# The 32 scatters of routed rows in pairs, each pair waiting until the pair before has landed

## The chip, the cores and the metric

The kernel runs on one core of a Trainium2 chip. The metric is the device time of one execution in microseconds (us); the kernel before was timed three times, and the median is what the changed kernel is held against. The profile is that of one further execution, recorded instruction by instruction.

## The reference

Two gated layers follow each other on 8 x 256 tokens of 128 numbers. The change touches the last part of the second layer, the mixture of experts:

```
x  = x + s0 * silu(local_attention_ffn(layernorm(x)))        # layer 0, s0 from a linear recurrence
xn = layernorm(x)
s  = attention(xn)                                           # 16 heads of 8, causal
probs = softmax(xn @ router_w.T + router_b);  top_w, top_e = top_k(probs, 2);  top_w /= sum(top_w)
for each expert e of 16:                                     # F = 256
    h = silu(xn @ w1[e].T) * (xn @ w3[e].T);  y = h @ w2[e].T
    yn = layernorm(y) * ln_g[e] + ln_b[e]
    out += where(top_e == e, top_w, 0).sum(-1) * yn
x  = x + s * silu(out)
```

Every token thus needs two of the 16 experts, and the kernel computes only these.

## The kernel before

The 2048 tokens are 16 tiles of 128 (`NT = 16`). The program has three parts. **Part a** goes through four turns of four tiles: layer 0, and beside it the second layer's attention of the turn before. **Part b** (the section `LAST` of the planner's order) does the second layer's attention for the last turn, transposes the weights of the 16 experts as they are loaded, and works out the routing. **Part c** takes 48 tiles of 128 routed rows (`CT = 48`) through the experts. Between the parts all engines meet: each drains and adds one to `b_over`, and goes on when it has reached 4.

The hand-over from part b to part c goes through device memory. `XG` (`xg_scratch`) has 48 x 128 places for rows. VectorE (DVE) works out, for every token and each of its two experts, the place of its row, and writes these 32 columns of indices to `POSU` (line 1718). GpSimd (POOL) then copies each token's normalized row to its two places: 16 tiles times 2 indirect DMAs of 128 rows, 64 KB each (lines 1944 to 1947). Each adds 16 to the semaphore `scattered` when it has landed. Nothing of POOL's work follows in part b but its drain; all its other work of part b is queued ahead of the scatters. POOL's queue is in program order.

The queue of SyncE (SP) issues the loads of the expert weights in part b, three of 128 KB per expert into a ring of four (lines 808 to 812). Each next expert waits until TensorE (PE) has transposed the expert four before it. Then it issues two loads of 1 MB (line 814), waits until all 32 scatters have landed (line 817) and until part b is over on all engines (line 818), and loads the rows back from `XG` (line 824); PE's first instructions of part c wait for that load. So whichever ends last in part b, PE's and DVE's chain (which ends in the matmuls "dests" and the cast to `DEST`, lines 1651 to 1653) or POOL's scatters, sets the start of part c.

In part c POOL scatters the experts' outputs to a second scratch, `YT` (`yt_scratch`), one indirect DMA of 64 KB for each of the 48 tiles (line 1918). In part b the order of the items on PE, ScalarE (ACT), DVE and POOL comes from a planner; it ranks the routing step that writes the indices as if 45 us of work stood behind it (`PLACED, SENDING`, lines 130 and 312), which stands for the scatters. The change leaves that as it is. A helper (line 1208) issues all of ACT's activations and another (line 841) many of the matmuls, so that their rows share a line; lines 884 and 926 are the transposes of the attention's probabilities and their products with the values, line 1136 and 1143 the transposes of expert weights.

Of the kernel before, what the change touches and what calls it, by code (L numbers as in the profile page):

```python
# [485 lines left out]
def gated_layers(nc, ins, out):  # L486
    ctx = ExitStack()
    with ctx:
# [3 lines left out]
        def sem(name):  # L492
            return ctx.enter_context(nc.semaphore(name))
# [191 lines left out]
        zeroed, scattered = sem("zeroed"), sem("scattered")  # L685
# [1127 lines left out]
        def _(pool):  # L1813
# [128 lines left out]
            pool.wait_ge(zeroed, 16 * CT // 4)  # L1942
            pool.wait_ge(pos_done, 1)
            for t in range(NT):
                for k in range(2):
                    G.indirect_dma_start(XG, bass.IndirectOffsetOnAxis(POSU[:, k, t:t + 1], 0), XN1ALL[:, t, :], None)\
                        .then_inc(scattered, 16)
# [56 lines left out]
```

## Time and profile before

| | us |
|---|---|
| three runs | 882.73, 886.46, 886.53 |
| median | 886.46 |
| span of the profiled execution, first to last instruction | 918.4 |
| that span less the median | 31.9 |

No other time of the profiled execution is recorded than its span; what lies around a span (start and end of a program) comes on top. The profiled execution was therefore at least 31.9 us longer than the median of the timed ones, which is 3.6%. Busy shares of the span: PE 77%, DVE 70%, ACT 54%, POOL 43%. These are means over three parts with different limits; the part that the change touches runs from about 680 us to 795 us of the span, and is read from its own rows. Times below are from the start of the span.

### The profile page before, as it was taken

The numbers are of one execution on the slowest core, as the hardware profiler recorded it, in microseconds if no ns is written. First come the engines' busy times: TensorE is split into PE (matmuls) and PEld (weight loads), VectorE is DVE, ScalarE is ACT, GpSimd is POOL, SyncE is SP. The second block draws the span as 40 slices with busy tenths as digits, with TensorE's granted clock in tenths as the row PEclk, the third lists the DMA queues.
The fourth block names the chain that finished last, engine by engine and source line by source line (L and its number), as shares of the span: only waits on it lengthen the run. The fifth ranks groups of instructions, "written<-read, shape, count | busy, mean of one in ns | idle before, by whom it ended". The sixth has DMA issues, their size and how long they took to land.

```text
span 918.4 us, 20712 instructions
## 1 busy us (share of the span) xinstructions
PE 708.3 (77%) x7336; PEld 530.8 (58%) x7351; DVE 642.1 (70%) x1521; ACT 496.9 (54%) x893; POOL 392.0 (43%) x470
## 2 busy tenths in 40 slices
PE   4688887689899867998997798999859309798830
PEld 1456554457676734676675466658646207698830
DVE  5586776697869775977986797787658325476645
ACT  2444555465666753656676566655726205487711
POOL 7351633560714063434412760480041750068880
PEclk9789999899999997999999999999978759799975
DMA  8600000000000000000000000000023313122104
GB/s 206 177 1 1 1 1 1 1 1 3 1 2 1 2 1 3 2 1 2 1 2 1 1 1 2 1 2 2 1 87 87 119 42 128 36 70 70 62 35 146
DMA packets 43839, 30.03 MB, mean 33 GB/s; under 512 B 7650, under 2 KB 41692, under 8 KB 43484
## 3 DMA queue, kind: packets, MB, share of 16 engines
q1 hardware_dynamic: 39932, 23.17, 8.7%
q0 software_dynamic: 2560, 5.25, 1.5%
q8 instruction: 64, 1.05, 0.5%
q10 hardware_dynamic: 1248, 0.28, 0.2%
q14 instruction: 35, 0.29, 0.1%
HBM read 18.98 MB, written 9.44 MB: 31 GB/s over the span
## 4 chain that ended last, share of the span: by engine, by line
PE 38%; DVE 24%; issue 13%; POOL 13%; ACT 6%; another core or an unknown queue 4%; DMA 1%; DVEq 1%; POOLq 0%; ACTq 0%; SPq 0%
PE psM L841 14%; DVE arena L1538 5%; PE psO L926 4%; ACT arena L1208 4%; DVE PR L1426 4%; PE psT L884 4%; POOL yt_scratch L1918 3%; PE psS L875 3%; PE psS L911 3%; POOL arena L1895 3%; POOL arena L1892 3%; POOL RS L1871 2%; DVE MX L1420 2%; DVE arena L1546 2%
## 5 line engine op out<-in xcount | busy, mean ns | idle before, releaser
L841 PE MATMUL psM<-arena 128*128 128x128 f32 (+7 forms) x1168 | 267.9, 372 | 44.1 <-DVE arena L1538 25.3
L1208 ACT ACTIVATE arena<-psT 128x512 f32<-128x512 f32 (+2 forms) x296 | 150.8, 530 | 153.9 <-PE psT L1003 37.1
L841 PEld LDWEIGHTS psM<-arena 128*128 128x128 f32 (+5 forms) x1168 | 155.5, 190 | 93.0 <-DVE arena L1538 38.1
L1208 ACT ACTIVATE arena<-psM 128x512 f32<-128x512 f32 (+2 forms) x168 | 88.3, 543 | 114.3 <-PE psM L841 113.3
L1420 DVE TENSOR_REDUCE MX<-psS 128x4 f32<-128x512 f32 (+1 forms) x160 | 102.7, 682 | 62.5 <-issue 24.0
L1870 POOL TENSOR_SCALAR RS<-MV 128x2 f32<-128x2 f32 x56 | 14.4, 256 | 293.2 <-DVE MV L1574 167.5
L1892 POOL TENSOR_TENSOR arena<-arena,powm 128x8 f32<-128x8 f32 x64 | 109.9, 1717 | 5.3
L1208 ACT ACTIVATE PR<-PR 128x512 f32<-128x512 f32 x160 | 94.6, 626 | 21.1 <-DVE PR L1426 20.9
L1426 DVE TENSOR_TENSOR PR<-psS,MX 128x512 f32<-128x512 f32 x160 | 102.1, 678 | 0.0
L884 PE MATMUL psT<-ident,PR 128*128 128x128 f32 x640 | 94.3, 282 | 5.4 <-ACT PR L1208 1.9
L884 PEld LDWEIGHTS psT<-ident,PR 128*128 128x128 f32 x640 | 74.9, 145 | 34.1 <-issue 27.0
L1895 POOL TENSOR_TENSOR arena<-arena 128x512 f32<-128x512 f32 x64 | 85.7, 1339 | 0.0
L1538 DVE TENSOR_TENSOR arena<-psM,arena 128x512 f32<-128x512 f32 x128 | 81.7, 679 | 0.0
L1208 ACT ACTIVATE arena<-arena 128x768 f32 (+3 forms) x61 | 46.6, 763 | 49.9 <-DVE arena L1806 30.0
L1546 DVE TENSOR_TENSOR arena<-arena 128x512 f32<-128x512 f32 x64 | 55.1, 878 | 15.3 <-POOL arena L1895 15.2
L1891 POOL TENSOR_SCALAR arena<-arena 128x8 f32<-128x8 f32 x64 | 17.9, 280 | 104.6 <-DVE arena L1525 104.3
L1208 ACT ACT_TABLE_LOAD x43 | 55.2, 1283 | 10.0 <-PE psT L965 9.3
L1525 DVE TENSOR_REDUCE arena<-arena 128x8 f32<-128x512 f32 x64 | 43.4, 678 | 21.0 <-ACT arena L1208 20.6
L1003 PE MATMUL psT<-ident,arena 128*128 128x128 f32 x256 | 40.8, 287 | 19.9 <-DVE arena L1546 19.8
L911 PE MATMUL psS<-arena 32*128 32x256 f32 (+1 forms) x512 | 55.7, 346 | 0.0
L1918 POOL DMA_INDIRECT yt_scratch<-arena,DEST x48 | 49.7, 1036 | 12.1 <-issue 7.3
L1906 POOL TENSOR_SCALAR arena<-arena,lanem 128x256 f32<-128x256 f32 x32 | 29.2, 934 | 55.8 <-ACT arena L1208 55.8
(198 smaller groups left out, 1163.8 us busy)
## 6 DMA issues: line engine op xcount, KB each, us to landing
arena<-in_L_ffn_w SPq DMA_DIRECT2D x50, 128.0 KB
xg_scratch<-zeros SPq DMA_DIRECT2D x12, 256.0 KB, 3.7
arena<-xg_scratch SPq DMA_DIRECT2D x12, 256.0 KB
arena<-yt_scratch SPq DMA_DIRECT2D x4, 512.0 KB, 5.3
arena<-in_L_ffn_wqkv SPq DMA_DIRECT2D x2, 768.0 KB, 5.0
arena<-in_L_ffn_ln_g SPq DMA_DIRECT2D x1, 1024.0 KB, 5.3
arena<-in_L_ffn_ln_b SPq DMA_DIRECT2D x1, 1024.0 KB, 8.5
out<-arena SPq DMA_DIRECT2D x4, 256.0 KB, 2.2
```

What stands on the lines that cost most here:

```text
L841: return nc.tensor.matmul(o, lhsT, rhs, start=start, stop=stop)
L884: last = nc.tensor.transpose(bank[:, c * P:(c + 1) * P], PR[:, m % 4, c * P:(c + 1) * P], ident[:])
L911: last = nc.tensor.matmul(Sb[i][:, c * keys:(c + 1) * keys], QL[r, b, lane, qt * P:(qt + 1) * P], KT1[r, b * SEQ:b * SEQ + keys], start=False,
L1208: return nc.scalar.activation(o, i, f, **kw)
L1420: V.tensor_reduce(maxima[i], scores[i], AX, ALU.max).then_inc(dstep, 1)
L1426: V.tensor_tensor(PR[:, (n + i) % 4, :].rearrange("p (s k) -> p s k", s=ns), scores[i], maxima[i].unsqueeze(2).broadcast_to([P, ns, 512 // ...
L1525: V.tensor_reduce(SS[:, m % 4, :], SQ[:, m % 2, :].rearrange("p (h d) -> p h d", h=8), AX, ALU.add).then_inc(ss_done.sem(m), 1)
L1538: last = V.tensor_tensor(dst.rearrange("p (h d) -> p h d", h=8), src, RT[:, 2 * l + n % 2, x, t % 2, :].unsqueeze(1) .broadcast_to([P, 8, ...
L1546: V.tensor_tensor(r1, r1, RN[:, m % 4, :].unsqueeze(2).broadcast_to([P, 8, DH]), ALU.mult)\
L1892: G.tensor_tensor(RN[:, m % 4, :], RN[:, m % 4, :], powm[:, 0:8], ALU.pow)
L1895: G.tensor_tensor(r1, r1, r2[:, :, ::-1, :], ALU.add).then_inc(rope_sum.sem(m), 1)
L1918: G.indirect_dma_start(YT, bass.IndirectOffsetOnAxis(DEST[:, tile:tile + 1], 0), YO[:, tile % OUT_RING, :], None)\
```

## The change

Ahead of the two scatters of every tile but the first, POOL waits until all scatters issued so far have landed. Nothing else differs.

```diff
             pool.wait_ge(zeroed, 16 * CT // 4)
             pool.wait_ge(pos_done, 1)
             for t in range(NT):
+                if t:
+
+                    pool.wait_ge(scattered, 16 * 2 * t)
                 for k in range(2):
                     G.indirect_dma_start(XG, bass.IndirectOffsetOnAxis(POSU[:, k, t:t + 1], 0), XN1ALL[:, t, :], None)\
                         .then_inc(scattered, 16)
```

On POOL, at the scatters, the difference of the two orders is this (the names are those of the section above; the scatters' line is 1949 in the changed kernel; the piece stops after the third pair):

```order
 L1906 TENSOR_SCALAR arena<-arena,lanem 128x256 x3
-L1946 DMA xg_scratch<-XN1ALL,POSU 6144x128 [waits pos_done,zeroed]
-L1946 DMA xg_scratch<-XN1ALL,POSU 6144x128 x31
+L1949 DMA xg_scratch<-XN1ALL,POSU 6144x128 [waits pos_done,zeroed]
+L1949 DMA xg_scratch<-XN1ALL,POSU 6144x128
+L1949 DMA xg_scratch<-XN1ALL,POSU 6144x128 [waits scattered]
+L1949 DMA xg_scratch<-XN1ALL,POSU 6144x128
+L1949 DMA xg_scratch<-XN1ALL,POSU 6144x128 [waits scattered]
```

No instruction moved; the first scatter of each of 15 pairs now carries a wait, where 31 scatters stood without one.

On SP, at the end of part b, this stands in both kernels, and it is who waits for the scatters:

```order
L812 DMA arena<-in_L_ffn_w 128x256
L814 DMA arena<-in_L_ffn_ln_g 128x16x128
L814 DMA arena<-in_L_ffn_ln_b 128x16x128
L824 DMA arena<-xg_scratch 128x4x128 [waits b_over,scattered]
L824 DMA arena<-xg_scratch 128x4x128
```

All weight loads stand ahead of the wait for the scatters, and the load of the routed rows behind it; nothing moved here.

## Rows read from the trace of the kernel before

**Rows 1.** The page: span, and busy tenths of 40 slices of 23 us.

```profile
span 918.4 us, 20712 instructions
PE   4688887689899867998997798999859309798830
POOL 7351633560714063434412760480041750068880
PEclk9789999899999997999999999999978759799975
```

**Rows 2.** Chain that ended last, end of part b: start us, us, what.

```profile
792.31 1.56 PE psM L841 x32
...
794.43 0.21 DVE DEST L1653
794.63 0.39 DVEq L1753
795.03 0.02 issue
795.04 0.02 SPq L818
795.06 0.04 issue
795.10 2.76 DMA arena<-xg_scratch
```

**Rows 3.** The same chain, 718 to 757 us.

```profile
718.76 2.49 another core or an unknown queue
...
723.18 31.99 another core or an unknown queue
755.17 0.02 issue
755.19 0.02 ACT arena L1208
755.21 1.38 another core or an unknown queue
```

**Rows 4.** Stretches: PE, PEld, DVE, ACT, POOL busy us (instructions), clock, DMA share, GB/s.

```profile
700.00:720.00 20.00, 17.32 (x178) 12.64 (x180) 18.84 (x38) 13.77 (x27) 7.11 (x7) 1.00 0.43 126
720.00:725.00 5.00, 2.74 (x22) 2.01 (x20) 0.63 (x1) 1.91 (x4) 3.78 (x5) 0.73 0.49 147
725.00:755.00 30.00, 0.00 (x0) 0.00 (x0) 4.73 (x7) 0.00 (x0) 20.51 (x22) 0.50 0.16 55
755.00:795.00 40.00, 34.41 (x505) 28.07 (x506) 22.36 (x36) 19.49 (x38) 0.00 (x0) 0.90 0.22 74
```

**Rows 5.** Timeline of DVE, PE and ACT: start us, us, instruction, [idle before it <-releaser].

```profile
740.52 0.69 DVE L1420 TENSOR_REDUCE MX<-psS 128x4 f32<-128x512 f32 x1 [19.89 <-issue]
755.19 0.60 ACT L1208 ACTIVATE arena<-psT 128x512 f32<-128x512 f32 x1 [32.01 <-remote]
755.93 1.09 PE L1136 MATMUL psT<-ident,arena 128*128 128x128 f32 x4 [31.52 <-ACT arena L1208]
```

**Rows 6.** Timeline of DVE and POOL, the first scatters and the last.

```profile
710.00 0.17 DVE L1718 CAST POSU<-arena 128x32 uint32<-128x32 f32 x1
...
711.06 1.23 POOL L1946 DMA_INDIRECT xg_scratch<-XN1ALL,POSU  x1 [12.17 <-DVE POSU L1718]
712.60 0.96 POOL L1946 DMA_INDIRECT xg_scratch<-XN1ALL,POSU  x1 [0.30 <-issue]
...
750.96 0.96 POOL L1946 DMA_INDIRECT xg_scratch<-XN1ALL,POSU  x1 [0.30 <-issue]
```

**Rows 7.** The scatters' line (ns min/median/max), and POOL's drain behind them.

```profile
L1946 POOL DMA_INDIRECT xg_scratch<-XN1ALL,POSU x32: 954/959/1233, 711.1 to 751.0; - x32
...
L1948 POOLq DRAIN  x1: 17969/17969/17969, 736.6 to 736.6; - x1
```

**Rows 8.** Chain that ended last, the last scatter of part c and SP behind it.

```profile
896.56 2.22 DMA yt_scratch<-arena,DEST
898.78 0.02 issue
898.80 0.03 SPq L827
898.83 0.04 issue
898.87 3.75 DMA arena<-yt_scratch
```

**Rows 9.** Timeline of POOL in part c.

```profile
888.93 1.13 POOL L1918 DMA_INDIRECT yt_scratch<-arena,DEST  x1 [0.20 <-issue]
890.36 0.97 POOL L1918 DMA_INDIRECT yt_scratch<-arena,DEST  x1 [0.30 <-issue]
```

## The prediction

> **What bounds the kernel now.** I read the page first, for where the span has a hole, then the chain that ended last around that hole, then tables of stretches, and last the timelines of the engines at both ends of the scatters. The page shows one slice, the 33rd (735 to 758 us), in which PE does nothing, with the clock at half, while POOL is busy half the time [rows 1]. The question is which of two things ends part b: the chain of PE, ACT and DVE, or POOL's scatters.
>
> In the profiled execution it is the chain. SP's wait for the end of part b is ended by DVE's drain at 795.0 us, and the load of the routed rows starts at 795.10 [rows 2]. The scatters were over long before: the last was issued at 750.96 [rows 6]. Taken by itself this says that the scatters have 40 us to spare, and that a change that only slows them is free. But the same chain holds one piece of 31.99 us, from 723.18, that the trace can put down to nobody [rows 3]. In the 30 us from 725 to 755 PE and ACT execute nothing and DVE 4.73 us, while POOL goes on scattering [rows 4]. ACT resumes at 755.19 after 32.01 us of "remote", PE right behind it [rows 5].
>
> Did the timed runs have this hole? The profiled span is 31.9 us above their median, and the hole is 31.99 us. Nothing else in the chain is a single wait of such a size. I take it that the timed runs have no hole, or hardly any, and that the profile must be read with it taken out. The Trainium skill has a rule for how that could be: by "NOTIFIC — the notification-queue block", section 7.1, the block that writes the profiler's records never loses one inside itself but holds the engines back instead. By that rule the hole would belong to recorded executions alone; no row here shows those records being written, and the sum and the chances below rest on the two lengths only.
>
> **Taking the hole out.** Part c then starts at 795.10 - 31.99 = 763.11 us. At most the two short unassigned pieces, 2.49 and 1.38 us, go with it [rows 3], which gives 759.24. Less than 918.4 - 886.46 = 31.94 can't go, since a timed run is no shorter than its own span: that end is 763.16. The span becomes 918.4 - 31.99 = 886.4, and the median is 886.46. The scatters' own end doesn't move with the hole: they start when DVE has written the indices, at 710.17 [rows 6], and stream until 750.96 + 0.96 = 751.92. POOL's drain, which begins at 736.64 and lasts 17.97, ends at 754.61 [rows 7]. So without the hole POOL is through 763.11 - 754.61 = 8.5 us ahead of the chain, not 40. That is all the cover there is.
>
> **What the change adds.** Fifteen waits, each until the pair ahead has landed. Behind the waiting scatter on POOL's queue stand the remaining scatters and the drain, nothing else; for these SP waits, and through `b_over` all engines. Now a scatter is issued every 0.96 + 0.30 = 1.26 us [rows 6], whether the one before has landed or not. The new period of a pair is the sum of four terms.
>
> - The wait's end until the first scatter starts. The row nearest to it is the first scatter, which waits for the cast to `POSU`: 711.06 - 710.17 = 0.89 us [rows 6]. The other end is SP, which goes on 0.09 us after a scatter's landing, 898.78 to 898.87 [rows 8]. I take 0.89, since it is the same engine and instruction.
> - The first scatter of a pair: 0.96 in the stream, 1.23 at the start of it [rows 6], 1.13 in part c behind other work [rows 9]. I take 1.13.
> - The gap to the second: 0.30 [rows 6].
> - The second from issue to landing: 2.22 us, the last scatter of part c, same size and kind [rows 8].
>
> The sum is 0.89 + 1.13 + 0.30 + 2.22 = 4.54 us for a pair that took 2 x 1.26 = 2.52. The low end is 0.09 + 0.96 + 0.30 + 2.22 = 3.57, the high end 0.89 + 1.23 + 0.30 + 2.22 = 4.64.
>
> The first pair starts as before, at 711.06, and lands at 711.06 + 1.23 + 0.30 + 2.22 = 714.81. Fifteen periods later the last lands: 714.81 + 15 x 4.54 = 782.91. POOL's drain ended 754.61 - (750.96 + 2.22) = 1.43 us after the last landing, and I keep that: part b is over on POOL at 784.3. That is 784.3 - 763.1 = 21.2 us after the chain. The scatters become what ends part b, and the difference goes to the end in full, since the load of the rows, and PE behind it, start from there [rows 2].
>
> Hence 886.46 + 21.2 = **907.7 us**. Ends: 714.81 + 15 x 3.57 + 1.43 = 769.8 against a chain at 763.16 gives +6.6, 893.1; 714.81 + 15 x 4.64 + 1.43 = 785.8 against 759.24 gives +26.6, 913.1. Against the profiled span as it stands the same sum would give something else, the first rival.
>
> What else the longer stream touches: it lies beside PE's weight loads for 30 us more. From 720 to 725 such loads ran beside the scatters at 147 GB/s in all, and the scatters need 64 KB in 1.26 us of it, some 52 [rows 4, 6]; they now need less, 29. I cost this at nothing; what hides it is the ring of four experts. PE idles from 763 to 784 and starts part c at a low clock: in the stretch with nothing to do the clock was granted at 0.50, the lower of its two levels [rows 4]. Part c opens with a wait for the load in both kernels, so I add nothing; if the clock's rise is late it is a loss of a microsecond or two inside the range.
>
> **The rivals.**
>
> *The hole is in the timed runs, and the gaps close it.* Then the profile is to be taken as it stands: part b ends at 795.10, the scatters hold the other engines up, and pairs with a pause let them go on. The end of part b becomes the later of chain and scatters, 784.3, so the change gains 795.1 - 784.3 = 10.8 us: 875.7 us, and at the short period 795.1 - 769.8 = 25.3, 861.2. It decides where the timed runs have more than 21.2 us of hole. For it: the hole starts 12 us into the stream (723.18 against 711.06) and ends 1.99 us after the last landing (755.17 against 750.96 + 2.22 = 753.18) [rows 3, 6, 8]. Against it: the two lengths above; and room on the DMA engines was not short, their share was 0.16 in the hole [rows 4]. The Trainium skill speaks against it as well: by "DMA: Bandwidth & Descriptors", section "SWDGE vs HWDGE vs iDMA", each DMA engine takes turns between the queues of software- and hardware-made transfers, so that a stream of scatters shouldn't lock out the others. The 147 GB/s beside the scatters agree with that. Chance 0.12.
>
> *The waits are hidden.* The period would have to be under (763.1 + 4.4 - 1.43 - 714.81) / 15 = 3.42 us, or the chain later in timed runs than I read it. The landing of 2.22 would have to be shorter for rows sent to `XG`, and the wake-up near nothing. That ends within 0.5% of the median (4.4 us, about what a measurement can tell from no change here): about 886, 882 to 891. Chance 0.08.
>
> *The hole is in the timed runs and lasts as long as the stream.* PE's chain then resumes 2 us after the last landing, with 795.1 - 755.2 = 39.9 us still to do: 782.9 + 2.0 + 39.9 = 824.8, which is 29.7 later than 795.1: 916 us. For it: that is how the hole ended. Against it: the new pauses, in each of which no scatter is under way, and the same two lengths. Chance 0.08.
>
> **How the numbers follow.** The forecast, 893 to 913, has 0.72. The range takes in the hidden case, 0.08, and leaves out the gain and the longest loss, 0.20 together: 883 to 914. Slower by over 0.5%: 0.72 + 0.08 = 0.80; same 0.08; faster 0.12.
>
> **What the profile after would show.** The scatters in 16 pairs with a pause ahead of each, some 4.5 us apart, the last near 780 us instead of 751; a pause of about 2 us between a pair's second issue and the next first one means that period and price are right. SP's wait at the end of part b ended by POOL or a scatter, not by DVE. PE idle between its last matmul of part b and the load of the rows. If the trace after still has a hole of tens of us in the scatters' stretch, what the pauses do to it can be read there, and only the timed median tells whether it counts. The prediction is wrong if pairs come every 3.4 us or faster, if PE's chain in the timed runs ends after 780, or if the median drops, which would mean that the hole had been in the timed runs.

## The result, and the profile after

| | us |
|---|---|
| before, median of four runs beside the changed kernel | 886.50 |
| changed kernel, median of four runs | 910.49 (907.71 to 911.96) |
| ratio, with its 95% interval | 1.0288 (1.0243 to 1.0334) |
| recorded execution of the changed kernel: time, span | 909.7, 907.5 |

The changed kernel is slower by 24.0 us; 907.7 was forecast. What lies around the span is 909.7 - 907.5 = 2.2 us here.

The page of the changed kernel, with the same rows as [rows 1] (slices of 22.7 us):

```profile
span 907.5 us, 20712 instructions
PE   3788887689899966998998699889976993298830
POOL 7351633560705064525231670283024235268880
PEclk8699999899999997999999899899996997599975
```

PE still idles in one place, but the place is a different one: the 34th and 35th slice, after its last matmul of part b. The table of the same stretches as [rows 4] (PE, PEld, DVE, ACT, POOL busy us, clock, DMA share, GB/s) shows it:

```profile
720.00:725.00 5.00, 4.47 (x76) 3.58 (x79) 4.93 (x8) 4.03 (x8) 2.27 (x2) 1.00 0.64 187
725.00:755.00 30.00, 26.20 (x394) 20.45 (x387) 22.39 (x34) 17.54 (x35) 12.48 (x12) 1.00 0.39 125
755.00:785.00 30.00, 3.40 (x84) 2.98 (x75) 2.27 (x6) 0.15 (x1) 13.39 (x14) 0.62 0.10 33
```

From 725 to 755 us, where the profiled execution of before had its hole, PE is busy 26.20 us and DVE 22.39. From 755 to 785 PE and DVE finish part b (3.40 and 2.27 us), and then only POOL goes on. The timeline of POOL, answering [rows 6], shows the pairs:

```profile
713.02 1.23 POOL L1949 DMA_INDIRECT xg_scratch<-XN1ALL,POSU  x1 [12.39 <-DVE POSU L1718]
714.56 0.96 POOL L1949 DMA_INDIRECT xg_scratch<-XN1ALL,POSU  x1 [0.31 <-issue]
717.60 0.95 POOL L1949 DMA_INDIRECT xg_scratch<-XN1ALL,POSU  x1 [2.07 <-DMA xg_scratch<-XN1ALL,POSU]
...
744.25 0.96 POOL L1949 DMA_INDIRECT xg_scratch<-XN1ALL,POSU  x1 [7.13 <-DMA xg_scratch<-XN1ALL,POSU]
...
780.30 0.96 POOL L1949 DMA_INDIRECT xg_scratch<-XN1ALL,POSU  x1 [0.31 <-issue]
```

Ahead of each pair POOL is idle, and what ends the idle time is the landing of the pair before. The line's own summary says the same (idle time, times): 31.1 us in 15 waits.

```profile
  DMA xg_scratch<-XN1ALL,POSU: 31.1, 15
  DVE POSU L1718: 12.4, 1
  issue: 4.9, 16
```

The chain that ended last, answering [rows 2, 3], goes through the scatters:

```profile
732.42 2.22 DMA xg_scratch<-XN1ALL,POSU
734.64 0.27 issue
734.90 0.96 POOL xg_scratch L1949
735.86 0.30 issue
736.16 7.83 DMA xg_scratch<-XN1ALL,POSU
743.99 0.27 issue
...
778.80 5.16 POOLq L1951
784.03 2.74 DMA arena<-xg_scratch
```

A period without disturbance can be added up here: 0.96 and 0.30, then 2.22 from the second issue to its landing, then 0.27 until the next start, 3.75 us. One landing took 7.83. SP's wait for the end of part b, which DVE's drain ended before, is now ended by POOL's drain, after 45.1 us (waited for, times, longest):

```profile
SPq L818 <- POOLq L1951: 45.1, 1, 45.1
```

### The profile page after: what moved, and what is told of

Its sections match the earlier page's. It is cut to its first block, busy times and chain, and to the rows that moved or that the text cites. A ratio compares the mean times of both kernels' runs of the same rounds, so it can differ in the third digit from the quotient of the medians.

```text
span 907.5 us, 20712 instructions
## 1 busy us (share of the span) xinstructions
PE 709.3 (78%) x7336; PEld 529.9 (58%) x7351; DVE 641.7 (71%) x1521; ACT 497.9 (55%) x893; POOL 393.1 (43%) x470
## 4 chain that ended last, share of the span: by engine, by line
PE 32%; DVE 24%; POOL 16%; issue 15%; ACT 6%; DMA 6%; POOLq 1%; DVEq 1%; ACTq 0%; SPq 0%
PE psM L841 13%; DVE arena L1538 5%; DMA xg_scratch<-XN1ALL,POSU 4%; ACT arena L1208 4%; DVE PR L1426 4%; POOL yt_scratch L1918 3%; POOL arena L1892 3%; PE psT L884 3%; PE psS L875 3%; PE psO L926 3%; POOL arena L1895 3%; POOL RS L1871 3%; PE psS L911 2%; DVE MX L1420 2%; DVE arena L1546 2%
## 5 line engine op out<-in xcount | busy, mean ns | idle before, releaser
L841 PE MATMUL psM<-arena 128*128 128x128 f32 (+7 forms) x1168 | 271.6, 375 | 42.4 <-DVE arena L1538 23.3
L1949 POOL DMA_INDIRECT xg_scratch<-XN1ALL,POSU x32 | 32.3, 1008 | 48.4 <-DMA xg_scratch<-XN1ALL,POSU 31.1
```

Source lines behind the costliest of these rows:

```text
L841: return nc.tensor.matmul(o, lhsT, rhs, start=start, stop=stop)
```

## The experiments

Two theories about the loss of 24 us stand against each other in most of them. One: a wait lays bare the time from issue to landing; part b ends with the later of the scatters and the chain of PE and DVE. The other: the wait as such, or the mere length of the stream, costs.

**The kernel before, recorded again.** Whether the hole of 32 us belongs to the kernel decides what the profile of before can be used for.

> The kernel before, unchanged, recorded once more, to see whether the hole of 32 us in the scatters' stretch is there again. If it belongs to a rare execution: span about 884 us, no piece over 5 us put down to nobody, scatters from 711 to 754, part b ended by DVE near 760. If it belongs to every recorded execution of a stream without pauses: span near 918 again, with the hole at the same place. If it is in the timed runs too, they would have to be the longer ones, which they are not.

Its time was 885.17 us, its span 883.0. The chain at the end of part b has no piece put down to nobody:

```profile
754.16 3.70 PE psO L926 x128
757.87 1.56 PE psM L841 x32
...
760.19 0.39 DVEq L1753
...
760.60 0.02 SPq L818
...
760.66 2.64 DMA arena<-xg_scratch
```

So the hole belongs to that one execution. None of the 32 runs of before that stand beside the experiments (881.99 to 891.67 us; longest span 889.5) was anywhere near 918, and none of the other eight recorded executions has such a hole. What made it stays open. With this trace the comparison is plain: SP's load of the rows starts at 760.66 before and at 784.03 after, 23.4 us later. The rest of the program, from that load to the end, takes 883.0 - 760.66 = 122.3 us before and 907.5 - 784.03 = 123.5 after. The spans differ by 24.5.

Part a isn't equally long in the recordings, so that part b is best counted from SP's first load of it. That load in SP's timeline, in the execution of [rows 1], in the kernel before recorded again, and in the changed kernel:

```profile
676.88 0.89 SPq L810 DMA_DIRECT2D arena<-in_L_ffn_w  x2
680.53 0.89 SPq L810 DMA_DIRECT2D arena<-in_L_ffn_w  x2
678.62 0.89 SPq L810 DMA_DIRECT2D arena<-in_L_ffn_w  x2
```

From there to the load of the rows it is 795.10 - 676.88 = 118.2 us with the hole, 760.66 - 680.53 = 80.1 without it, and 784.03 - 678.62 = 105.4 in the changed kernel. Part b became 25.3 us longer by the change. The chain of PE and DVE did not: its last cast ended 80.0 us after that first load, in the kernel before recorded again 79.7.

The scatters and the drain behind them show how little cover there was (ns min/median/max, first and last start; the drain's start and length):

```profile
L1946 POOL DMA_INDIRECT xg_scratch<-XN1ALL,POSU x32: 954/958/1966, 714.9 to 755.7; - x32
L1948 POOLq DRAIN  x1: 18822/18822/18822, 740.6 to 740.6; - x1
```

POOL's drain ends at 740.6 + 18.8 = 759.4, DVE's at 760.58. The scatters had 1.2 us to spare in this recording.

**The wait every four scatters.**

```diff
-                if t:
+                if t and t % 2 == 0:
 
                     pool.wait_ge(scattered, 16 * 2 * t)
```

> The wait ahead of every second tile only: groups of four scatters, 7 waits in place of 15. Theory (a wait lays bare issue to landing plus the wake-up, 3.76 - 2.52 = 1.24 us each where nothing else is on the DMA engines, more beside the weight loads; part b ends with the later of the scatters and the chain of PE and DVE): last landing near 763 to 768, part b over at 765 to 769 against 761, so 4 to 8 us slower than before, about 892 us. Rival (the length of the stream itself, or crowding, slows PE's chain): half the loss of the pairs, 12 us, 898.

898.18 us, ratio 1.0144 (1.0092 to 1.0196), 13 us slower: the figure of the rival. But the chain shows why, and it is not PE's chain, whose last cast ended at 760.4 as before. The scatters ended part b (chain):

```profile
755.94 0.95 POOL xg_scratch L1949
756.90 0.31 issue
757.20 2.23 DMA xg_scratch<-XN1ALL,POSU
759.44 0.27 issue
...
765.75 7.67 POOLq L1951
...
773.43 0.02 SPq L818
...
773.49 2.62 DMA arena<-xg_scratch
```

Part b was over 12.8 us later than in the kernel before recorded again. It adds up from the waits: 7 x 1.23 = 8.6 us, 5.5 for four landings of 2.8 to 5.7 us in place of 2.22 while weights and the two 1 MB loads were under way, less 1.2 of cover, is 12.9. My figure was too low because I had reckoned with 5 to 6 us of cover, and there was 1.2, and because these landings came out at the upper end.

**The wait every eight scatters.**

```diff
-                if t:
+                if t and t % 4 == 0:
 
                     pool.wait_ge(scattered, 16 * 2 * t)
```

> The wait ahead of every fourth tile: 3 waits. Theory: the scatters end 4 to 6 us later than without waits, which is about what PE's chain covers: 886 to 889 us, the same as before. Rival (loss in proportion to the waits, no cover): 3/15 of 24 = 4.8 us, 891.

890.33 us, ratio 1.0071 (1.0044 to 1.0098): 5 us slower, above the 886 to 889 of the theory, so three waits are not covered. SP's load starts at 765.21, 4.5 us later, ended by POOL's drain. It is the rival's figure again, and with so little cover the loss is indeed nearly in proportion to the waits. But three waits at 1.23 us less the cover are only 2.5; in this recording the rest is for the most part single scatters that took long (1.65 us once, 1.96 twice) and only 0.9 us is landings.

**A wait for the pair before the last.** Two semaphores count the pairs in turn, and SP waits for both.

```diff
             for t in range(NT):
+                if t > 1:
+                    pool.wait_ge(scattered[t % 2], 16 * 2 * (t // 2))
                 for k in range(2):
...
-                        .then_inc(scattered, 16)
+                        .then_inc(scattered[t % 2], 16)
```

> 14 waits, but each for the pair before the last, counted on two semaphores in turn; so a pair is always under way while the next is issued. Theory: that pair has landed (1.26 us after its second issue, when 2.52 us of the next pair's issue have passed), the stream stays at 2.52 us a pair, last landing 753 to 757, time as before, 886 to 888. Rival (the wait as such costs POOL a restart of 0.3 to 0.9 us or more whatever it waits for): 14 times 0.5 to 1.5, part b over 4 to 17 us later, 890 to 905.

888.09 us, ratio 1.0015 (0.9986 to 1.0044): no difference that can be measured, which leaves room for up to 0.4%. Of its 14 waits only two held POOL up, 3.6 us together, both beside the two 1 MB loads (idle time of the scatters' line):

```profile
  issue: 8.8, 29
  DMA xg_scratch<-XN1ALL,POSU: 3.6, 2
```

At the other twelve waits the gap to the next scatter stayed at 0.30 us, as without a wait. The wait as such costs nothing here; a wait costs what it must really wait for. Quite free it was not in the recorded execution: the last scatter was issued at 759.67, so that it landed at about 761.9 and not by 757, as the theory had it; POOL's drain and not DVE's ended part b, and SP's load came at 763.42, 2.8 us later than without waits.

**A wait ahead of every scatter.**

```diff
                 for k in range(2):
+                    if t or k:
+                        pool.wait_ge(scattered, 16 * (2 * t + k))
```

> Every scatter but the first waits until all before it have landed: 31 waits in place of 15. Theory (a wait turns 1.26 us from issue to issue into 2.22 to the landing and 0.27 to the next start, so 1.23 us each; landings beside the weight loads take longer, 9 us in all with 15 waits; about 1 us of cover): 31 x 1.23 - 1 + 9 to 18 = 46 to 55 us slower than before, 931 to 940. Rival (the loss comes from the stretch in which the weight loads run, and the waits after it are cheap): under 40 us, below 925.

932.18 us, ratio 1.0541 (1.0497 to 1.0584), 48 us slower, inside what the theory gave. The chain's last scatters come every 2.49 us, 2.22 to the landing and 0.27 to the next start:

```profile
795.31 2.22 DMA xg_scratch<-XN1ALL,POSU
797.53 0.27 issue
797.79 2.22 DMA xg_scratch<-XN1ALL,POSU
```

These rows lie after the weight loads, and a wait costs 2.49 - 1.26 = 1.23 us in them too, which excludes the rival (cheap waits after the loads). The kernels together, by their recorded executions; the fifth column is counted from SP's first load of part b:

| waits | first to last scatter issue, us | more than without, per wait | SP's load of the rows at | part b until that load, us | ratio to before |
|---|---|---|---|---|---|
| 0 | 40.8 | | 760.66 | 80.1 | 1 |
| 3 | 47.0 | 2.1 | 765.21 | 85.2 | 1.0071 |
| 7 | 54.6 | 2.0 | 773.49 | 92.8 | 1.0144 |
| 15 (the change) | 67.3 | 1.8 | 784.03 | 105.4 | 1.0288 |
| 31 | 89.1 | 1.6 | 806.49 | 127.3 | 1.0541 |
| 14, for the pair before the last | 44.6 | 0.3 | 763.42 | 82.5 | 1.0015 |

In the rows of 3 to 31 waits, part b is longer by what the stream is longer, less 1.1 to 1.2 us of cover. The price of a wait is 1.23 us by itself; what comes on top, 2.5 to 10 us in all, is landings that took longer and, with 3 waits, mostly scatters that did.

**The two loads of 1 MB first.** The landing of 7.83 us began at 736.16, and SP had issued the loads of the experts' scales and shifts at 735.40 and 736.08. This kernel is the changed one with these two loads ahead of the expert weights (the three lines taken out below are cut after the first).

```diff
             sp.wait_ge(a_over, ENGINES)
+            for m, w in enumerate(("ln_g", "ln_b")):
+                sp.dma_start(W13[:, :, 2 * FE + m * D:2 * FE + (m + 1) * D], ins[f"L1_ffn_{w}"].partition_broadcast(P))\
+                    .then_inc(ld_gb, 16)
...
-            for m, w in enumerate(("ln_g", "ln_b")):
```

> The changed kernel, with the two loads of 1 MB (the scales and shifts of the experts' layernorm) issued at the start of part b, ahead of the experts' weights, and not behind them in the midst of the scatters. Theory (one pair's landing took 7.83 us beside them and not 2.22): no landing over 4 us, part b over 5 to 6 us earlier than in the changed kernel, about 905 us. Rival (the DMA engines' work is the same wherever it stands, or the long landing came from elsewhere): 910, no difference.

906.72 us, ratio 1.0236 (1.0185 to 1.0287). By the times alone that can't be told from the change's 1.0288, the intervals overlap. The recorded execution, one of each kernel, shows what the move does: the longest landing is down to 4.0 us, and the scatters take 63.4 us from first to last issue in place of 67.3 (times to landing, min/median/max, here and in the changed kernel):

```profile
DMA to landing us min/median/max: 2.2/2.2/4.0
```

```profile
DMA to landing us min/median/max: 2.2/2.2/7.8
```

3.9 us is less than the 5 to 6 expected, since the same pair, the sixth, still took 3.98 us to land; just ahead of it SP issues the last expert's weights in both kernels. The other landings that are slow beside weight loads are those of the first three pairs in both. In this execution part a was 5.4 us longer than in that of the changed kernel (SP's first load of part b at 684.07), so that its own time, 911.66, is above the median; counted from that load, the load of the rows comes 101.9 us later in place of 105.4.

**The same move without waits.** The block of three lines is moved as above, in the kernel before.

```diff
             sp.wait_ge(a_over, ENGINES)
+            for m, w in enumerate(("ln_g", "ln_b")):
...
-            for m, w in enumerate(("ln_g", "ln_b")):
```

> The same move in the kernel before, without any wait. Theory (a slow landing costs only where somebody waits for it; part b is ended by the chain of PE and DVE): 885, within 0.5% of before; the experts' first weights come some 8 us later, which the chain's own pace may or may not hide, at most 8 us slower. Rival (the two loads hold up the scatters' stream itself): 2 to 5 us faster.

884.22 us, ratio 0.9992 (0.9967 to 1.0016): no difference that can be measured. The scatters take 40.8 us from first to last issue, as before: the loads don't hold up POOL's issuing. A slow landing costs where somebody stands and waits for it.

## Why the prediction was right, point by point

**The hole in the timed runs: rightly left out, but by a match of lengths that was luck.** The second recording has no hole, and neither have the timed runs. Read with the hole in it, the profile would have given a gain of 10.8 us, and that rival is dead. The third rival (a hole as long as the stream) fell too. But the argument was that the surplus of the span, 31.9 us, equals the hole, 31.99, and part b lost more than the hole. Counted from SP's first load, part b of that execution was 118.2 - 80.1 = 38.1 us longer than in the second recording. Its part a happened to be 3.7 us shorter and its part c 1.0 longer, which makes the 35.4 by which the two spans differ; against the span of a median run that comes to about 34.

**The chain: too late by 6.1 us.** This is the largest term that was mis-sized. 763.11 is 86.2 us after part b's first load, where the second recording has 80.1; even the low end, 759.24, is 82.4. Taking out the 31.99 us left in what was lost around the hole and behind it. 3.2 us of that lie just around it, where the two short pieces are. The rest is PE at a lower clock, granted at 0.51 and 0.57, near the lower of its two levels, and not at 1.00. Here are two groups of 128 matmuls of the chain behind the hole, 4.91 and 5.37 us, where the second recording has 3.70 (above, at 754.16), then the stretches around them (clock third from the end), and the second recording's stretch for the later one:

```profile
757.36 4.91 PE psO L926 x128
786.94 5.37 PE psO L926 x128
```

```profile
755.00:760.00 5.00, 3.73 (x56) 3.39 (x60) 0.00 (x0) 2.72 (x5) 0.00 (x0) 0.51 0.02 3
787.00:791.00 4.00, 4.00 (x88) 4.00 (x92) 1.51 (x2) 0.00 (x0) 0.00 (x0) 0.57 0.01 4
```

```profile
754.00:758.00 4.00, 3.83 (x133) 3.67 (x134) 1.81 (x3) 0.02 (x1) 2.39 (x2) 1.00 0.11 37
```

Ahead of the first, PE had done nothing for 31.5 us. The later one isn't tied to the hole: the kernels with 3 waits and with the loads moved and no wait took 5.2 us at the same place, so that the chain, and the cover with it, varies by 1.6 us between recordings without a hole.

**The cover: too large for the same reason.** I had 8.5 us between POOL's drain and the chain; there were 1.2. 6.1 us of the difference are the chain. The other 1.1 are the scatters': POOL's drain ended 77.7 us after part b's first load in the profiled execution of before and 78.9 in the second recording, mostly because one scatter near 753 us takes about 2 us (below). The hole had pushed the DVE instructions beside it behind the scatters, so that this couldn't show. The first scatter starts 34.2 to 34.8 us after part b's first load in all nine recordings. "The waits are hidden" was further off than its 0.08, and the two experiments with few waits came out at 13 and 5 us, not at 4 to 8 and 0 to 3.

**The period of a pair: about right, by two errors that nearly cancel.** I took 4.54 us. From the first pair's landing at 717.33 to the last at 780.30 + 2.22 = 782.52, the mean is 4.35. But ten of the 15 pairs came 3.75 us after the one before. Two terms were mis-sized. The wake-up was 0.27, not 0.89: the first scatter's 0.89, which stands in the trace after as well (712.13 to 713.02), is not the price of a wait but of the first scatter. And the first of a pair took 0.96, not 1.13. That made the sum 15 x 0.79 = 11.9 us too large. The step "I cost this at nothing", on the stream beside the weight loads, failed the other way. I asked only whether the scatters would slow the loads; PE's chain, 0.3 us longer, shows that they hardly did. The loads slow the landings: the other five periods are 9.7 us longer than 3.75 each, 9.1 of that landings and the scatter of 2 us, 5.6 in the one pair beside the two 1 MB loads. Before the change nobody waited for a single landing, so that no row of before could show it. A better wake-up alone would have made the forecast worse.

**The sum.** The last landing was forecast at 782.91 and came at 782.52, but that closeness is luck too, since part a was 1.7 us longer in the recording after: counted from part b's first load it came 2.1 us earlier than forecast, 103.9 and not 106.0. So the sum had the chain 6.1 us too late and POOL's end 2.0 too late (105.4 for 107.4), and part b grew by 25.3 us where 21.2 was forecast. The mechanism is the one that was forecast; that the time came within 3 us rests in part on errors that work against each other in the loss.

**What ends part b, and that the loss goes to the end: right.** POOL's drain ends the wait, and the 25.3 us that part b grew carry through: with a part a 1.9 us shorter and a part c 1.1 longer they are the 24.5 by which the spans differ. I had named a microsecond or two for part c, which PE enters after 28.5 us without work. That the 1.1 are the price of this idle time is not shown. They arise in the first 9 us of part c, where the clock was lower (0.73 in the first 16 us, 0.89 in the kernel before recorded again); but the kernel with the loads moved and no waits, which waits only for the load, also loses 1.0 in those 9 us, and the one with 31 waits, which idles longest, 0.4.

## What to carry to other kernels

A wait for a transfer's landing costs the landing each time: where issues overlapped at 1.26 us, waiting made it 2.49. To bound what is in flight, wait for the one before the last; that made no difference that could be measured here. And before a profile is used to say how much cover a transfer has, hold its span against the timed runs, and if it is too long, record again: the hole turned 1.2 us of cover into 40, and with the hole's own length taken out there still stood 8.5.

## What the runs showed of the hardware that was not expected

A 64 KB scatter's landing, 2.22 us from its issue when alone, took up to 7.83 us beside two hardware-queue loads of 1 MB. The mean DMA share of 0.39 from 725 to 755 us hides why: around that landing the DMA engines were 0.92 busy, at 296 GB/s (changed kernel, the last two numbers of the row):

```profile
736.00:744.00 8.00, 7.61 (x108) 5.72 (x100) 4.56 (x9) 4.88 (x11) 0.96 (x1) 1.00 0.92 296
```

In the kernels with 7, 14 and 31 waits such a landing took 5.66, 6.54 and 6.61 us, at shares of 0.84 to 0.97. In all four it came 7.7 to 8.4 us after SP issued the second 1 MB load, whenever the scatter itself was issued; with 3 waits a scatter issued 0.34 us ahead of the first load landed in 2.82. Full engines are not the only cause of a slow landing: 3.42 us in the changed kernel (from 723.72) and the 3.98 with the loads moved came at shares of 0.18 and 0.24. What slowed these stays open.

POOL's making of a scatter's transfers is not constant either. In every recorded execution in which DVE's four comparisons of line 1743 (1.2 us each) ran beside the scatters, one scatter took 1.9 to 2.0 us and not 0.96, with 3 waits two did, and in the kernel that waits for the pair before the last a second took 1.71; here from the kernel before recorded again, POOL first, then DVE:

```profile
752.21 0.95 POOL L1946 DMA_INDIRECT xg_scratch<-XN1ALL,POSU  x1 [0.30 <-issue]
753.47 1.97 POOL L1946 DMA_INDIRECT xg_scratch<-XN1ALL,POSU  x1 [0.30 <-issue]
```

```profile
751.11 4.62 DVE L1743 TENSOR_TENSOR arena<-arena 128x1024 bf16<-128x1024 f32 x4
```

In [rows 7], where the hole had moved these comparisons behind the scatters, no scatter took more than 1.23. Why one is stretched and the next ones beside the same comparisons are not was not tried.

The hole itself, 32 us in which PE, ACT and nearly DVE stood while the scatters went on, appeared in one of the nine executions whose traces are kept. That the recording caused it was argued, not shown.
